# Moving the multiplication of the features by v from GpSimd to ScalarE in a two-layer graph attention kernel

## What is computed

```python
h = (node_features @ W_proj.T).reshape(B, N, H, dh)
s_left = jnp.einsum('bihd,d->bih', h, wl)
s_right = jnp.einsum('bjhd,d->bjh', h, wr)
scores = s_left[:, :, None, :] + s_right[:, None, :, :] + adjacency[..., None] * we
scores = jax.nn.leaky_relu(scores, negative_slope=0.2)
scores = scores + (NEG * pad)[..., None]
attn = jax.nn.softmax(scores, axis=2)
agg = jnp.einsum('bijh,bjhd->bihd', attn, h).reshape(B, N, D)
out = jax.nn.leaky_relu(node_features + agg + bias, negative_slope=0.5)
x = _layernorm(x + out, axis=-1)
```

## Time and profile before

| | |
|---|---|
| median of 3 runs | 1983.24 us (1981.75 to 1984.76) |
| the profiled execution's own time | 1981.11 us |
| its span | 1979.2 us |
| busy, of the span | PE 1795.4, DVE 1821.9, ACT 1646.4, POOL 1866.3 us |
| granted TensorE clock, mean | 0.992 of full speed |
| main loop, POOL's first to last tile | 75.39 to 1959.30 us |

### The profile page before, as it was taken

The page is one execution under the profiler, slowest core; times in us unless marked ns, Lnnn a source line. Parts: engine busy times, 40 slices in busy tenths (PEclk is TensorE's granted clock), DMA queues, the critical chain, the costliest instruction groups (busy, mean ns, idle before and its releaser), DMA issues.

```text
span 1979.2 us, 34310 instructions
## 1 busy us (share of the span) xinstructions
PE 1795.4 (91%) x11080; PEld 875.2 (44%) x11080; DVE 1821.9 (92%) x3413; ACT 1646.4 (83%) x3895; POOL 1866.3 (94%) x663
## 2 busy tenths in 40 slices
PE   7799999999999999899999999999999999878885
PEld 6544444444444444445444444444444444333332
DVE  3699999999999999999999999999999999999997
ACT  6788887899888898888988889888887898676674
POOL 3599999999999999999999999999999999999995
PEclk9899999999999999999999999999999999999999
DMA  3232315233243243333233331333315233333310
GB/s 100 73 115 91 102 50 157 83 114 106 66 138 99 81 120 100 94 113 99 79 120 100 86 119 58 121 121 91 102 54 156 81 113 91 102 96 96 102 54 11
DMA packets 138090, 190.63 MB, mean 96 GB/s; under 512 B 22328, under 2 KB 56504, under 8 KB 137912
## 3 DMA queue, kind: packets, MB, share of 16 engines
q1 hardware_dynamic: 137912, 188.44, 31.8%
HBM read 179.77 MB, written 8.65 MB: 95 GB/s over the span
## 4 chain that ended last, share of the span: by engine, by line
POOL 28%; ACT 20%; PE 19%; issue 17%; DVE 15%; SPq 0%; DMA 0%; ACTq 0%; DVEq 0%; POOLq 0%
POOL X L501 26%; PE psum L1217 15%; DVE X L1102 11%; ACT E L773 4%; PE psum L1396 3%; ACT psum L776 3%; ACT pen L734 3%; ACT squares L642 2%; DVE X L1091 2%; POOL haug L484 1%; ACT blk L590 1%; ACT blk L563 1%; ACT x1s L670 1%; ACT o_sb L670 0%; ACT act_T L563 0%
## 5 line engine op out<-in xcount | busy, mean ns | idle before, releaser
L501 POOL TENSOR_TENSOR X<-RHO,E 128x1536 f32<-128x1536 f32 (+1 forms) x512 | 1779.3, 3506 | 41.8 <-ACT E L773 35.3
L1102 DVE SCALAR_TENSOR_TENSOR X<-psum,s_j,X 128x512 f32<-128x512 f32 x2048 | 1397.4, 741 | 78.8 <-POOL X L501 68.0
L1217 PE MATMUL psum<-X,haug 128*33 128x512 f32 x4096 | 978.6, 598 | 8.2 <-ACT accU L752 4.6
L1396 PEld LDWEIGHTS psum<-ident,adj_sb 128*128 128x128 f32 x2048 | 285.9, 140 | 561.8 <-DVE X L1102 429.1
L1396 PE MATMUL psum<-ident,adj_sb 128*128 128x128 f32 x2048 | 430.6, 291 | 101.3 <-DVE X L1102 97.7
L773 ACT ACTIVATE E<-psum,we_s 128x512 f32<-128x512 f32 x512 | 395.5, 772 | 139.0 <-PE psum L1217 137.1
L1217 PEld LDWEIGHTS psum<-X,haug 128*33 128x33 f32 x4096 | 195.0, 110 | 431.7 <-issue 390.6
L776 ACT ACTIVATE psum<-psum,we_s 128x512 f32<-128x512 f32 x512 | 380.7, 744 | 0.0
L1217 PE MATMUL psum<-sgn_ident,pen 128*128 128x128 bf16 x2048 | 374.7, 219 | 0.0
L734 ACT ACTIVATE pen<-adj_sb,pen_bias 128x512 bf16<-128x512 f32 x512 | 366.8, 717 | 1.0 <-PE psum L1217 0.2
L1091 DVE TENSOR_TENSOR X<-psum,E 128x512 f32<-128x512 f32 x496 | 334.0, 673 | 3.6 <-ACT RHO L563 2.2
(11 more groups left out here) (231 smaller groups left out, 1547.5 us busy)
## 6 DMA issues: line engine op xcount, KB each, us to landing
adj_sb<-in_adj_dram SPq DMA_DIRECT2D x128, 1024.0 KB, 5.2
RHO<-rho_scratch SPq DMA_DIRECT2D x31, 1024.0 KB, 9.7
out_dram<-o_sb SPq DMA_DIRECT2D x32, 256.0 KB, 2.3
xg<-in_x_dram SPq DMA_DIRECT2D x28, 256.0 KB, 5.3
blk<-in_adj_dram SPq DMA_DIRECT2D x56, 64.0 KB, 5.1
X<-in_x_dram SPq DMA_DIRECT2D x2, 256.0 KB, 3.0
W_sb<-in_L_gnn_W_dram SPq DMA_DIRECT2D x4, 64.0 KB, 2.1
X<-in_adj_dram SPq DMA_DIRECT2D x4, 64.0 KB, 2.8
```

Of the source, the lines that this page charges most:

```text
L501: Q.tensor_tensor(X[m % NX][:, 0:heads, :], RHO[:, g % 2, 0:heads, :], bc(E[m % NE][:], 1, [P, heads, GROUP]), ALU.mult).then_inc(B_pool, 1)
L1102: ins = V.scalar_tensor_tensor(slot[:, h, :], TA[m % NT], s[:, k, h:h + 1], slot[:, h, :], ALU.mult, ALU.max)
L1217: return T.matmul(o, l, r, start=start, stop=stop)
L1396: T.matmul(o, adj_sb[c][:, t, at:at + P], ident[:], is_transpose=True, start=True, stop=False)
```

## The change

`make_haug` moves from POOL's list to ACT's. It now does one tile of nodes a call, in four instructions (one per head, 32 columns, the scale being v of that head, one number per partition). A body has 16 such calls: the table puts four calls each at slots 59 to 62, 62 to 65, 70 to 73 and 73 to 76. For the first graph four calls stand before ACT's work at tile 0, and four each at tiles 1, 2 and 3. The waits follow: `values` waits for each tile of nodes, `chain_h` for the four tiles that it overwrites. All tables have new numbers, among them `FOUR`.

```diff
-    FOUR = (11, 29)
+    FOUR = (22, 36)
...
-    AT_ACT = {"xT": (-24, -16, 2, 20), "wh0": (-23, -15, 6, 21), "wh1": (-21, -13, 9, 22),
...
+    AT_ACT = {"xT": (-24, -17, 2, 20), "wh0": (-23, -15, 5, 21), "wh1": (-22, -13, 8, 22),
...
-    AT_POOL = {"xb": (-24, -8, 20, 25), "r_shift": (5, 24, 39, 45), "haug": (58, 59, 62, 65)}
+          "h0": (10, 29, 46, 52), "h1": (11, 32, 49, 52), "haug": (59, 62, 70, 73)}
...
+    AT_POOL = {"xb": (-20, -7, 19, 23), "r_shift": (6, 21, 38, 45)}
...
-            def make_haug(nb, q):
-                if q == 0:
-                    pool.wait_ge(v_sb, nb + 1)
-                    if nb >= 2:
-                        pool.wait_ge(pv_done, BODY * (nb - 1))
-                rows = slice(q * CHUNK, (q + 1) * CHUNK)
-                Q.tensor_tensor(haug[nb % 2][:, rows, :, 0:DH], hb[:, rows, 0:D].rearrange("p t (h d) -> p t h d", h=H),
-                                bc(v_j[:, rows], 3, [P, CHUNK, H, DH]), ALU.mult).then_inc(haug_sb, 1)
...
-            for q in range(NC_):
-                make_haug(0, q)
...
             def chain_h(c, j):
                 act.wait_ge(h_ps[j], c + 1)
+                if c >= NB and j == 0:
+                    act.wait_ge(haug_sb, JT * (c // NB - 1) + CHUNK * (c % NB + 1))
                 if c % NB == 0 and j == 0 and c > 0:
-                    act.wait_ge(haug_sb, NC_ * (c // NB))
                     act.wait_ge(sig_sb, c // NB)
...
+            def make_haug(nb, k):
+
+                if k == 0:
+                    act.wait_ge(v_sb, nb + 1)
+                    if nb >= 2:
+                        act.wait_ge(pv_done, BODY * (nb - 1))
+                for h in range(H):
+                    ins = copy(haug[nb % 2][:, k, h, 0:DH], hb[:, k, h * DH:(h + 1) * DH], v_j[:, k, h:h + 1])
+                ins.then_inc(haug_sb, 1)
...
+                        if 0 <= n - AT_ACT["haug"][u] < CHUNK:
+                            make_haug(nb, CHUNK * u + n - AT_ACT["haug"][u])
...
             penalty(3)
+            for k in range(CHUNK):
+                make_haug(0, k)
             for m in range(-BODY // 2, 0):
                 host(m)
             make_hcol(0)
...
                 host(m)
+                if 0 < m < CHUNK:
+                    for k in range(CHUNK * m, CHUNK * (m + 1)):
+                        make_haug(0, k)
                 penalty(m + LEAD)
...
             def values(m):
                 g, k = divmod(m, JT)
-                if k % CHUNK == 0 and g % NB == 0:
-                    pe.wait_ge(haug_sb, NC_ * (g // NB) + k // CHUNK + 1)
+                if g % NB == 0:
+                    pe.wait_ge(haug_sb, JT * (g // NB) + k + 1)
+                if k == 0 and g % NB == 0:
                     pe.wait_ge(hden_sb, g // NB + 1)
```

More of the change, by code:

```diff
@@ L42, in build_program @@
     U = range(NB)
-    FOUR = (11, 29)
+    FOUR = (22, 36)
     AT_SP = {"load": (-30, -23, -3, 9)}
-    AT_PE = {"xT": (-26, -20, 0, 18), "wh0": (-26, -17, 0, 18), "wh1": (-24, -16, 5, 19), "ST": (-11, 7, 20, 29),
+    AT_PE = {"xT": (-27, -22, 0, 18), "wh0": (-26, -18, 0, 18), "wh1": (-25, -16, 5, 19), "ST": (-11, 6, 20, 29),
           "oT": (-10, 10, 21, 32), "y1": (-9, 11, 22, 33), "y2": (-8, 12, 24, 34), "z0": (-7, 13, 25, 35),
[2 rows of a table removed]
-    AT_ACT = {"xT": (-24, -16, 2, 20), "wh0": (-23, -15, 6, 21), "wh1": (-21, -13, 9, 22),
[L54 to L57, removed]
@@ L58, in build_program @@
-    AT_DVE = {"max": (-20, -13, 12, 26), "rin": (-18, -6, 16, 27), "res": (1, 19, 30, 42)}
-    AT_POOL = {"xb": (-24, -8, 20, 25), "r_shift": (5, 24, 39, 45), "haug": (58, 59, 62, 65)}
[2 rows of a table added]
+    AT_ACT = {"xT": (-24, -17, 2, 20), "wh0": (-23, -15, 5, 21), "wh1": (-22, -13, 8, 22),
+          "logits": (-21, -13, 9, 24), "exp": (-19, -11, 13, 27), "soft": (-14, -5, 19, 30), "ST": (-9, 11, 23, 33),
+          "oT": (-7, 13, 24, 35), "y1": (-6, 14, 25, 36), "y2": (-5, 14, 26, 36), "ssq": (-4, 17, 28, 39),
+          "z_rstd": (0, 17, 29, 40), "r_rstd": (4, 20, 36, 45), "r_norm": (7, 24, 40, 49), "x1T": (8, 29, 46, 51),
+          "h0": (10, 29, 46, 52), "h1": (11, 32, 49, 52), "haug": (59, 62, 70, 73)}
@@ L60, in build_program @@
+    AT_DVE = {"max": (-20, -13, 11, 26), "rin": (-16, -7, 14, 29), "res": (1, 19, 30, 43)}
+    AT_POOL = {"xb": (-20, -7, 19, 23), "r_shift": (6, 21, 38, 45)}
     ONCE_PE = {"rmT": 52, "Rb": 53, "rhoT": 55, "hsum": 56}
-    ONCE_ACT = {"diag": 55, "factors": 57, "rho": 58, "hcol": 61}
-    ONCE_DVE = {"rm": 52, "R4": 54, "lam": 55}
+    ONCE_ACT = {"diag": 55, "factors": 56, "rho": 58, "hcol": 62}
+    ONCE_DVE = {"rm": 53, "R4": 54, "lam": 55}
     ONCE_SP = {"rho": 49}
-    EPI_PE = {"back0": 2, "back1": 3}
+    EPI_PE = {"back0": 1, "back1": 3}
@@ L65, in build_program @@
     EPI_ACT = {"acc": 2, "prelu": 7, "rstd": 10, "norm": 15}
-    EPI_DVE = {"part0": 4, "part1": 5, "lky": 6}
-    EPI_POOL = {"shift": 15}
+    EPI_DVE = {"part0": 3, "part1": 5, "lky": 6}
+    EPI_POOL = {"shift": 13}
     EPI_SP = {"store": 15, "rho": 8}
@@ L514, in host @@
                             r_shift(c)
-                        if n == AT_POOL["haug"][u]:
-                            make_haug(nb, u)
             Q.memset(wlr[:], 0.0).then_inc(const_set, 1)
```

## The result

| | before | the change |
|---|---|---|
| median us | 1983.7 (1981.75 to 1984.76, 4 runs) | 2007.5 (2002.1 to 2012.6, 4 runs) |
| profiled execution, us | 1981.11 | 2002.13 |
| its span | 1979.2 | 2000.4 |
| mean granted clock of the runs | 0.992 (profiled run) | 0.987, 0.986, 0.983, 0.982 |

What follows compares the result with a forecast made beforehand. POOL was taken to set the main loop's pace, with ACT taking over for moments. 1981.11 + 11.8 (start) + 2 (six transitions) - 4 (seventh) = 1990.9; with the median 2.1 us above the profiled execution, forecast 1993, range 1975 to 2003.

Steps and rivals of the forecast that it cites:

- POOL's relief: Haug passes leaving POOL: 1.00 us each, four a graph, hidden for the first graph, at most 28.0 us for the others.
- The price of a copy: On ACT, a 32-column copy with a scale per partition takes 0.215 us; a graph's copies cost 13.8 us.
- The start: First graph's tiles: copies ahead of E on ACT make POOL start tile 5 at 108.8, +11.8 us once.
- the transition: From one graph to the next, mainly slots 58 to 75: ACT's added work turns POOL's relief there into waits for E.
- +0.8 + 0.1 - 0.6 = +0.3, six of them +2 us: Each full transition: stretch of slots 58 to 75 +0.8, POOL outside it +0.1, ACT's moved work returning -0.6.
- I have counted all of it as filled: ACT's 10.3 us of idle time in slots 58 to 75, assumed wholly filled by the added work.
- ACT waits as well: Rival: ACT's waits for PE and POOL in slots 58 to 75 stay, 2 us each time; 2005 us, chance 0.15.
- The lead: At slot 58, POOL's start behind ACT's, taken as 2.82 us and subtracted from ACT's 69.5 us of work.
- I take 0.6: The 46 slots outside the stretch: of the 0.9 us of work that ACT loses there, 0.6 comes back.
- The seventh transition: Bodies 6 and 7, no further graph to prepare: the copies fit and POOL saves its four passes, -4 us.
- at full TensorE clock: Body 3 before the change, 237.1 us: the engines' busy times were read at this clock.
- costed at nothing: Other table entries: moves without new work that shift pieces by a slot or two, put at no cost.

Runs made afterwards that it cites:

- one plain copy: The changed kernel with one plain copy of 128 columns per tile of nodes in place of four scaled ones, multiplication by v left out: 1956.7 us, ratio 0.9871.
- The start alone: The kernel before with only its first graph's copies moved to ACT, tables and other graphs unchanged: 1995.8 us, ratio 1.0068.
- the tables alone: The kernel before with only the change's new tables and `FOUR`, all haug passes left on POOL: 1977.6 us, ratio 0.9977.
- The old tables: The changed kernel with the tables and `FOUR` of the kernel before, copies on ACT at the change's slots: 2042.7 us, ratio 1.0299.

## Why the prediction was wrong

1. **POOL's relief: right.** 1.00 us a pass, hidden at the start, 28 us at most. With one plain copy on ACT most of it comes out: full bodies of 233.5 us in place of 237.2.
2. **The price of a copy: right.** 0.215 forecast, 0.212 measured. By the figures of the Trainium skill's "ScalarE: Activation LUTs" (What ACT_TABLE_LOAD costs) the estimates are 0.213, and 0.120 without the pointer. The trace agrees: plain copies of 32 columns measured 0.12.
3. **The start: right, but only in ACT's time.** Tile 3 at 99, tile 4 at 104.5, tile 5 at 108.8 were forecast; 99.2, 104.6 and 108.9 came. What I did not price is the clock: in that profile body 0 has a mean of 0.97, before 0.99. The start alone, measured over the whole run, cost 13.9 us.
4. **The step that failed is the transition**, "+0.8 + 0.1 - 0.6 = +0.3, six of them +2 us". The stretch cost 1.6 us in a clean transition and 3.7 in one with a dip, 11.5 in all six.
   - The mechanism was right (ACT's work above that of POOL and DVE in those 18 slots), its size wrong. ACT's own stretch was put at 69.5 us without idle time and took 71.2: 68.6 busy and 2.6 idle. The step that was wrong is "I have counted all of it as filled", the idle time of ACT. The waits that the forecast named (accU, x1T, the shift of the norm) did vanish under ACT's lateness. What stayed are waits of E for its bank, 2.0 us, because the 18 slots aren't one sum: ACT is overloaded in the slots 59 to 65 and 70 to 75, catches up between them and can't work ahead there. In size that is the rival "ACT waits as well", which put 2 us on each transition, though on other waits. The lead was 3.8 us instead of 2.8 and paid back one of these. In body 3 POOL's waits for E are 10.7 us, where 8 or 9 were forecast.
   - "I take 0.6" for what comes back outside the stretch: nearly nothing came back, 0.1 us in the bodies 1 to 5 together; only body 0 gave 1.3.
5. **The seventh transition**: -2.6, not -4, and body 6 lost 1.3 elsewhere, most of it a single wait for E of 1.04 us at slot 57. That loss belongs to the new tables: with the tables alone these slots of body 6 take 167.8 us, against 166.2 before and 167.5 in the change. Together 2.7 us.
6. **The clock was left out.** The prediction says "at full TensorE clock" and carries this over. In the profiled run one dip cost 2.1 us; the median lies 5.4 us above that run, at lower clocks. No term and no rival had it.
7. **The tables: costed at nothing.** Alone they bring 4 us, around the copies 35. Sums over stretches can't see this: ACT's work in its stretch is about the same with either set (68.2 and 68.6 us), and what the tables decide is in which slots it falls.

What was missed against 1993 adds up. Some 9.5 us are in the transitions with the one dip (11.5 against 2) and 2.7 in the last two bodies; less the 1.3 that body 0 gave, this makes 11 in the profiled run. That the median is 5.4 above it, where 2.1 had been allowed, makes the rest of 14.5.

## To carry to other kernels

An engine that is in nobody's way on average still has a queue. Before moving work to it, add up its work slot by slot against the pace of the engine that sets the time. Where the sum is higher, the relief elsewhere is lost, and where it is lower again, an engine that can't work ahead idles. Sharing the work between the two engines can do better than moving it: half of it on each was the fastest version here that computes everything, though a quarter on ACT brought nothing over the new tables alone. And where TensorE gets light slots, as here, its clock may fall in some executions, so look at the clocks of all runs and not only of the profiled one.

## What I had not expected of the hardware

- A dip of the clock inside a transition costs 2.1 us (70.5 against 68.4), or 2.6 (70.3 against 67.7), though the work of POOL and ACT, which set the pace there, takes as long in both (POOL 62.3 and 62.2 us, ACT 65.7 and 65.8 in the change). TensorE stands in their loop, and it is its busy time that grows (64.3 and 64.2 us against 61.6 and 61.4).
- The same program spreads by 0.5% in each of its two sets of four runs (2002.1 to 2012.6 and 1999.5 to 2008.8), its clock between 0.982 and 0.988. The old tables, whose profile has a dip in every full transition, hardly spread (2042.3 to 2043.1, clock 0.973 and 0.974). I read this as the chance of a dip spreading the runs, not the dip itself; the runs without a profile can't show it.
- A scale per partition nearly doubles a short ScalarE copy: 0.212 against 0.120 us for 32 columns of fp32.
